# A state-space scan: seven of sixteen states weighted in transposed form by ScalarE, VectorE's own states written over their decays

## What is computed

```python
dt = softplus(dt_low @ W_dt + b_dt)
A = -exp(A_log)                                  # (512, 16)
def step(h, inputs):                             # h: (4, 512, 16)
    dt_t, x_t, B_t, C_t = inputs
    h = exp(dt_t[..., None] * A) * h + (dt_t * x_t)[..., None] * B_t[:, None, :]
    y = einsum('bds,bs->bd', h, C_t)
    return (h, y)
y = (scan of step over 1024 tokens) + x * D
y = y * silu(z)
```

## Time and profile before

| | us |
|---|---|
| median of three runs | 4037.8 |
| lowest and highest run | 4034.0 and 4038.71 |
| the profiled execution | 4035.95 |
| its span, from the first to the last instruction | 4034.2 |

### The profile page before, as it was taken

One profiled execution on the slowest core, in us unless ns is written; L12 is line 12 of the kernel. 1 busy time (PEld: TensorE's weight loads), 2 busy tenths in 40 slices (PEclk: granted clock), 3 DMA queues, 4 the chain that ended last, 5 costly groups with the idle time before them and its releaser, 6 DMA issues. The chain is left out here.

```text
span 4034.2 us, 46003 instructions
## 1 busy us (share of the span) xinstructions
PE 3270.3 (81%) x16080; PEld 1802.9 (45%) x16080; DVE 2552.3 (63%) x3494; ACT 1604.3 (40%) x2988; POOL 1605.5 (40%) x1002
## 2 busy tenths in 40 slices
PE   8599997588888799789888798895466777667894
PEld 5244442355555455455555455332122222224773
DVE  8588884465665422365665322487799999997633
ACT  2277776155555311255555211355233333332100
POOL 4100000333333211233333211255799999995503
PEclk9799999699999899899999899998788888888897
DMA  5955550600000311100000321243615151512574
GB/s 161 138 68 68 68 68 28 200 17 21 17 21 21 105 54 47 55 17 21 19 19 17 87 63 61 89 143 127 252 46 214 52 219 45 216 52 97 188 217 122
DMA packets 286671, 356.64 MB, mean 88 GB/s; under 512 B 71940, under 2 KB 218220, under 8 KB 285804
## 3 DMA queue, kind: packets, MB, share of 16 engines
q1 hardware_dynamic: 272636, 329.96, 29.2%
q10 hardware_dynamic: 10736, 15.38, 1.1%
q0 software_dynamic: 3072, 8.39, 0.7%
HBM read 245.63 MB, written 107.48 MB: 88 GB/s over the span
## 5 line engine op out<-in xcount | busy, mean ns | idle before, releaser
L2265 POOL TENSOR_TENSOR H_feed<-H_ndu,H_bs 128x1024 f32<-128x1024 f32 x256 | 593.8, 2349 | 8.4 <-DMA H_cs<-between_bc 8.3
L2247 ACT ACTIVATE H_decay<-H_ndt,H_rate 128x1024 f32<-128x1024 f32 x256 | 286.2, 1118 | 548.8 <-DVE H_state L2319 460.0
L2348 PE MATMUL H_p_y<-H_part,H_minus 128*128 128x512 f32 x704 | 380.6, 672 | 133.1 <-DVE H_part L2296 133.0
L2319 DVE TENSOR_TENSOR_SCAN H_state<-H_decay,H_feed 128x1024 f32<-128x1024 f32 x176 | 404.5, 2298 | 49.7 <-POOL H_feed L2265 25.6
L709 ACT ACTIVATE B_probs<-B_p_exp,B_key_bias 128x512 f32<-128x512 f32 (+3 forms) x768 | 392.6, 582 | 107.6 <-PE B_p_exp L753 77.4
L643 DVE TENSOR_REDUCE B_part_max<-B_p_max 128x1 f32<-128x512 f32 (+3 forms) x768 | 375.3, 546 | 90.3 <-PE B_p_max L730 87.7
L1230 ACT ACTIVATE D_probs<-D_scores,D_neg,D_rq 128x256 f32<-128x256 f32 x512 | 281.6, 564 | 237.5 <-DVE D_neg L1148 237.5
L1089 POOL TENSOR_TENSOR D_rnorm<-D_norm,D_power 128x8 f32<-128x8 f32 x64 | 106.1, 1658 | 633.7 <-DVE D_norm L1107 633.7
L2348 PEld LDWEIGHTS H_p_y<-H_part,H_minus 128*128 128x128 f32 x704 | 140.5, 209 | 352.9 <-DVE H_part L2296 201.8
L727 PE MATMUL B_p_max<-B_k,B_q 100*128 100x512 bf16 (+3 forms) x768 | 255.1, 338 | 39.1 <-DMA B_key_bias<-in_key_bias 32.8
L1644 PE MATMUL E_p_ag<-E_hT,E_w 128*128 128x512 f32 x640 | 283.6, 603 | 2.0 <-ACT E_hT L1600 2.0
(11 more groups left out here) (256 smaller groups left out, 6702.4 us busy)
## 6 DMA issues: line engine op xcount, KB each, us to landing
H_bs<-between_bc SPq DMA_DIRECT2D x64, 512.0 KB, 9.6
H_cs<-between_bc SPq DMA_DIRECT2D x64, 512.0 KB, 11.1
B_q<-between_q_parts SPq DMA_DIRECT2D x96, 128.0 KB
B_k<-between_k_parts SPq DMA_DIRECT2D x96, 128.0 KB
D_base<-between_z SPq DMA_DIRECT2D x64, 128.0 KB, 2.2
between_z<-D_z SPq DMA_DIRECT2D x64, 128.0 KB, 1.7
E_rest<-between_z SPq DMA_DIRECT2D x16, 512.0 KB, 5.2
between_sz<-F_sz SPq DMA_DIRECT2D x8, 1024.0 KB, 4.2
```

Of the source, the lines that this page charges most:

```text
L2247: nc.scalar.activation(decay[:, n % 2, :], ndt[:, g % 2, :], ACT.Exp, scale=rate[:, m, s:s + 1]).then_inc(decayed, 1)
L2265: nc.gpsimd.tensor_tensor(feed[:, n % AHEAD, :], ndu[:, g % 2, :], bs[:, s, :], ALU.mult).then_inc(fed, 1)
L2319: nc.vector.tensor_tensor_scan(out, decay[:, n % 2, :], feed[:, n % AHEAD, :], 0.0, ALU.mult, ALU.add).then_inc(scanned, 1)
L2348: last = nc.tensor.matmul(p_y[:, c, :], minus[:, :], src[:, c * CHUNK:(c + 1) * CHUNK], start=False, stop=s == NS - 1)
```

## The change

The sixteen states of a tile now fall into three classes, by the string `CLASS = "TTDPTDTDPTDTPDTD"`: six D, three P, seven T.

- P (3, 8, 12) is what was called shared: scan to `handed`, product by GpSimd.
- D (2, 5, 7, 10, 13, 15) is VectorE's own. Its scan writes over the decay that it reads, `decay[:, n % 2, :]` in PSUM, and its product comes at once behind it. The tile `state` is gone. Decay n therefore waits for the product of n-2, where n-2 is a D.
- T (0, 1, 4, 6, 9, 11, 14): the scan goes to `turning` in SBUF, in three buffers. TensorE turns its eight 128x128 blocks into `p_T`, two banks of PSUM (`turn`). ScalarE copies them to `sT` with a scale per partition, which is now time, taken from C turned (`weigh`, eight ACTIVATEs of 128x128). TensorE multiplies each with `minus` as the moving operand, which turns it back, and adds it to `p_y` (`bring`, eight matmuls of 128 columns).

C for that is loaded once for each sequence as 16 rows of 1024 (`load_c`, 64 KB), turned by TensorE (`turn_c`, eight small transposes) and copied by ScalarE (`put_c`) in the last tile of the sequence before. Only the nine rows of C that are not T's are still spread to 128 partitions. The one semaphore `summed` becomes three, one for each class. TensorE's queue gets a new order: at step n the sum of P n-4, `bring` of T n-2, the sum of D n-1, `turn` of T n; the skip term comes with the first sum of its tile. On ScalarE the weighing of n-2 stands behind decay n. The tail now stands behind the scan of state 1.

```diff
+        CLASS = "TTDPTDTDPTDTPDTD"
-        cs = a.sb("cs", [P, NS, SEQ])
+        cs = a.sb("cs", [P, len(weighted), SEQ])
+        c_rows = a.sb("c_rows", [NS, SEQ])
+        cT = a.sb("cT", [P, 2, NB, NS])
+        turning = a.sb("turning", [P, 3, SEQ])
+        sT = a.sb("sT", [P, 2, NB, P])
-        state = a.ps("state", [P, SEQ])
+        p_T = a.ps("p_T", [P, 2, HB, P])
...
+            def weigh(n):
+                g, s = units[n]
+                i, k = g // XT, before["T"][n]
+                act.wait_ge(copied, 2 * use_of_c(i) + 2)
+                if k >= 2:
+                    act.wait_ge(t_summed, k - 1)
+                for h in range(2):
+                    act.wait_ge(turned, 2 * use_of(n) + h + 1)
+                    for b in range(HB):
+                        last = nc.scalar.activation(sT[:, k % 2, h * HB + b, :], p_T[:, h, b, :], ACT.Copy,
+                                                    scale=cT[:, i % 2, h * HB + b, s:s + 1])
+                    last.then_inc(copied, 1)
...
-                reached(act, scanned, n - 1)
+                if n >= 2 and kind[n - 2] == "D":
+                    act.wait_ge(parted, before["D"][n - 1])
+                else:
+                    reached(act, scanned, n - 1)
                 nc.scalar.activation(decay[:, n % 2, :], ndt[:, g % 2, :], ACT.Exp, scale=rate[:, m, s:s + 1]
                                      ).then_inc(decayed, 1)
+                if n == 1:
+                    put_c(0)
+                if n >= 2:
...
+                    if kind[n - 2] == "T":
+                        weigh(n - 2)
...
-                nc.vector.tensor_tensor(part[:, k % 3, :], state[:, :], cs[:, s, :], ALU.mult).then_inc(parted, 1)
+                nc.vector.tensor_tensor(part[:, k % 3, :], decay[:, n % 2, :], cs[:, weighted.index(s), :], ALU.mult
+                                        ).then_inc(parted, 1)
...
+                elif kind[n] == "T":
+                    if k >= 3:
+                        dve.wait_ge(turned, 2 * use_of([j for j in range(n) if kind[j] == "T"][k - 3]) + 2)
+                    out = turning[:, k % 3, :]
                 else:
+                    out = decay[:, n % 2, :]
                 nc.vector.tensor_tensor_scan(out, decay[:, n % 2, :], feed[:, n % AHEAD, :], 0.0,
                                              ALU.mult, ALU.add).then_inc(scanned, 1)
+                if kind[n] == "D":
+                    times_c(n)
-                if g and s == 2:
+                if g and s == 1:
                     tail(g - 1)
...
+            def turn(n):
+                u, k = use_of(n), before["T"][n]
+                pe.wait_ge(scanned, n + 1)
+                for h in range(2):
+                    pe.wait_ge(copied, 2 * u + h - 1)
+                    for b in range(HB):
+                        at = (h * HB + b) * P
+                        last = nc.tensor.transpose(p_T[:, h, b, :], turning[:, k % 3, at:at + P], ident[:, :])
+                    last.then_inc(turned, 1)
+
+            def bring(n):
+                g, s = units[n]
+                skip_term(g)
+                k = before["T"][n]
+                for h in range(2):
+                    pe.wait_ge(copied, 2 * use_of(n) + h + 1)
+                    for b in range(HB):
+                        last = nc.tensor.matmul(p_y[:, h, b * P:(b + 1) * P], sT[:, k % 2, h * HB + b, :], minus[:, :],
+                                                start=False, stop=False)
+                last.then_inc(t_summed, 1)
...
+            for n in range(NU + 5):
+                if 0 <= n - 4 < NU and kind[n - 4] == "P":
+                    k = before["P"][n - 4]
+                    pe.wait_ge(pool_parted, k + 1)
+                    add(n - 4, pool_part[:, k % 2, :], p_summed)
+                if 0 <= n - 2 < NU and kind[n - 2] == "T":
+                    bring(n - 2)
+                if 0 <= n - 1 < NU and kind[n - 1] == "D":
+                    k = before["D"][n - 1]
+                    pe.wait_ge(parted, k + 1)
+                    add(n - 1, part[:, k % 3, :], d_summed)
+                if n < NU:
+                    i = units[n][0] // XT + 1
+                    if units[n] == (XT * i - 1, NEXT_C) and i < SEQS:
+                        turn_c(i)
+                    if kind[n] == "T":
+                        turn(n)
```

More of the change, by code:

```diff
@@ L2140, in phase_scan @@
         NU = len(units)
-        shared = [s % 3 == 1 for g, s in units]
-        shared_before = list(accumulate(shared, initial=0))
-        own_before = [n - k for n, k in enumerate(shared_before)]
+        CLASS = "TTDPTDTDPTDTPDTD"
+        NB = SEQ // P
+        HB = NB // 2
+        NEXT_C = CLASS.index("P", NS // 2)
+        kind = [CLASS[s] for g, s in units]
+        before = {c: list(accumulate((k == c for k in kind), initial=0)) for c in "TDP"}
+        per = {c: CLASS.count(c) for c in "TDP"}
+        weighted = [s for s in range(NS) if CLASS[s] != "T"]
+        row_bytes = [16 if CLASS[s] == "T" else 32 for s in range(NS)]
         AHEAD = 4
@@ L2180, in reached, with use_of, use_of_c @@
                 eng.wait_ge(sem, value)
+        def use_of(n):
+            i = units[n][0] // XT
+            return before["T"][n] + 1 + i + (n % (XT * NS) > (XT - 1) * NS + NEXT_C and i + 1 < SEQS)
+        def use_of_c(i):
+            return before["T"][(XT * i - 1) * NS + NEXT_C] + i if i else 0
         @block.sync
@@ L2229, in _ @@
                     load_tail(g + 1)
+                if m == 0 and i + 1 < SEQS:
+                    load_c(i + 1)
                 if m == XT - 1 and i + 1 < SEQS:
@@ L2281, in _ @@
                     feeds(n)
-                if n >= 2 and shared[n - 2]:
+                if n >= 2 and kind[n - 2] == "P":
                     shared_product(n - 2)
@@ L2291, in times_c @@
                     dve.wait_ge(row_loaded[s], 32 * (i + 1))
-                k = own_before[n]
+                k = before["D"][n]
+                reached(dve, d_summed, k - 2)
                 dve.wait_ge(scanned, n + 1)
-                if k >= 3:
-                    dve.wait_ge(summed, [j for j in range(n) if not shared[j]][k - 3] + 1)
-                nc.vector.tensor_tensor(part[:, k % 3, :], state[:, :], cs[:, s, :], ALU.mult).then_inc(parted, 1)
+                nc.vector.tensor_tensor(part[:, k % 3, :], decay[:, n % 2, :], cs[:, weighted.index(s), :], ALU.mult
+                                        ).then_inc(parted, 1)
@@ L2331, in _ @@
         def _(pe):
[L2332 to L2346 removed]
+            started = set()
@@ new lines, in skip_term, with turn_c @@
+            def skip_term(g):
+                if g in started:
+                    return
+                started.add(g)
+                reached(pe, yg_ready, g)
+                pe.wait_ge(tail_loaded[g % 2], 32 * (g // 2 + 1))
+                for c in range(2):
+                    nc.tensor.matmul(p_y[:, c, :], skip_diag[:, tiles[g][1], :],
+                                     xs[:, g % 2, c * CHUNK:(c + 1) * CHUNK], start=True, stop=False)
+            def turn_c(i):
+                u = use_of_c(i)
+                pe.wait_ge(c_loaded, 16 * (i + 1))
+                for h in range(2):
+                    if u:
+                        pe.wait_ge(copied, 2 * u + h - 1)
+                    for b in range(HB):
+                        at = (h * HB + b) * P
+                        last = nc.tensor.transpose(p_T[:, h, b, 0:NS], c_rows[:, at:at + P], ident[0:NS, 0:NS])
+                    last.then_inc(turned, 1)
@@ L2347, in _, with add @@
+            def add(n, src, done):
+                g, s = units[n]
+                skip_term(g)
                 for c in range(2):
@@ L2349, in _ @@
                                             start=False, stop=s == NS - 1)
-                last.then_inc(summed, 1)
+                last.then_inc(done, 1)
+            pe.wait_ge(fixed, 48)
+            pe.wait_ge(diag_ready, 1)
+            turn_c(0)
+            for n in range(NU + 5):
[13 more added lines that the diff above has]
+                        turn_c(i)
+                    if kind[n] == "T":
+                        turn(n)
 EXPERTS = 32
```

80 lines of the change are left out of this document (40 added, 40 removed).

## The result

| | before | after |
|---|---|---|
| median, us | 4035.90 (4 runs) | 3928.52 (4 runs) |
| lowest and highest run | 4028.51 and 4038.71 | 3916.73 and 3932.89 |
| the profiled execution | 4035.95 | 3929.91 |
| its span | 4034.2 | 3928.1 |
| mean granted clock of TensorE | 0.918 | 0.942 |

The ratio is 0.9732, 95% interval 0.9713 to 0.9751. Of the 106.0 us between the two profiled executions 105.1 lie in the scan: from the start of the first scan (2856.84) to the end of the last tail (3586.99) it is 730.2 us, where it was 835.3. The forecast had 98.8 there (3590.2 - 2853.7 = 736.5 us for the stage) and 1.8 more ahead of the first scan, 100.6 in all.

A forecast was written before the change was run, and what follows sets the result against it. VectorE's (DVE's) own queue bounds the scan stage. 2853.7 + 16 x 44.4 + 15 x 1.35 + 1.5 + 4.3 = 3590.2 instead of 3690.8; 4035.95 - 100.6 + 1.9 = 3937 us, range 3926 to 3972.

The forecast's parts named there:

- a product followed by a scan 1.34 to 1.36: VectorE's queue: start-to-start time in us, read from the earlier timeline, that a product holds the queue before a scan.
- like a product: VectorE's queue: the tail, standing between two scans, should hold the queue 1.35 us.
- Cost 0; its cover is gone to a tenth.: GpSimd: feed 15 ready at 42.0, when scan 15 starts; 0.5 us per tile if an operation takes 0.04 more.
- The walk: GpSimd's queue followed through a tile: product 3 at 11.9, feed 15 thirteenth at 2.31 us each, ready at 42.0.
- first rival: GpSimd becomes the bound: 1 to 2 us per tile, 3953 to 3969 us; chance 0.17.
- The second rival: ScalarE holds decays back: 3.5 us weighings give 3951, table loads at each change 4015; chance 0.08.
- at 2.9 per weighing it is 11.7: ScalarE, states 0 and 1: with 2.9 us weighings decay 4 is done at 11.7, just when wanted; cost 0.
- The third rival: TensorE loses its clock at the tile's border: 4091 us, half about 4010; chance 0.06 whole, 0.05 part.
- The fourth rival: Transposes don't hold TensorE's clock; work after gaps before `bring` 4 and 9 starts low: 3959 us; chance 0.07.
- The fifth: D scan in place in PSUM pays the high end, 7.3 us per tile: 4054 us; chance 0.03.
- The wait at the third feed: Stage start: third feed at 2857.2 us leaves VectorE 1.5 us of the 2.8 it waited there.
- the longer end: Stage end: last product to last tail 4.3 us instead of 3.4, with `bring` 14 and the last sum in line.

The follow-up runs named there:

- late product: GpSimd's product of a P state placed one feed later in its queue (behind feed n+3 instead of n+2), against the changed kernel: 3908.14 us, ratio 0.9688.
- longer weighing: Twelve ACTIVATEs instead of eight per weighing, the extra four into an unread tile, against the kernel with the late product: 3997.58 us, ratio 0.9895.
- the run with the turnings moved: Kernel with the longer weighing, each turning from state 2 on put ahead of `bring` n-2 and the D sum in TensorE's queue: 3997.85 us, ratio 0.9908.
- all turnings moved: Nine-T kernel (two P, five D, late product), turnings from state 2 on put ahead of `bring` n-2 and the D sum: 4021.24 us, ratio 0.9965.

## Why the prediction was right

Forecast 3937, measured 3928.5; the range 3926 to 3972 holds it. The step from the engines' shares to DVE's queue as the price of the tile was right, and so was what leaves that queue. Two terms were off, in opposite directions, and that the time lies in the range is in part luck: with DVE's queue as it was measured and no wait for POOL it is 3908 (the run with the late product), below 3926.

**DVE's queue.** Forecast 45.75 us per tile, measured 44.27 where nothing else binds (the late product). The term that was mis-sized is "a product followed by a scan 1.34 to 1.36": the number was read rightly in the earlier trace rows, but there each own scan had to wait for the product that read `state`. The change takes this wait away, since a scan now writes elsewhere, and a product or a tail holds the queue 1.14 and 1.12 us. Seven times 0.21 is 1.5 us per tile. The list of waits before hardly named it, 0.5 us in the whole stage, its gaps being too short; the run with the wait put back showed what it costs there, 0.28 us each time. The trace before had both numbers side by side, right behind the tail of the earlier trace rows at 3021.40:

```profile
3022.52 1.21 DVE L2296 TENSOR_TENSOR H_part<-H_state,H_cs 128x1024 f32<-128x1024 f32 x1
3023.87 2.30 DVE L2319 TENSOR_TENSOR_SCAN H_state<-H_decay,H_feed 128x1024 f32<-128x1024 f32 x1
```

The product of state 2 does not wait for the tail and starts 1.12 us behind it; the scan waits for the product and starts 1.35 us behind it. The prediction gave the tail 1.35, "like a product". The prediction counted what the change removes in instructions, and missed what it removes in waits between two instructions of one engine.

**POOL.** "Cost 0; its cover is gone to a tenth." The walk named the place, the scan of state 15, and the chain, the product of state 3 and twelve operations behind it, rightly. With a slower DVE it even holds: with the wait put back, at 46.3 us per tile, POOL's wait is gone. With DVE faster it binds, 0.87 us per tile. This is the first rival's mechanism, smaller than its low end of 1 us, and a consequence of the first error: 44.26 + 0.87, and two waits of 1.4 for a decay in fourteen tiles, is 45.3, the measured tile. The forecast was too high by 0.49 us per tile, 7 us in fourteen. A walk with a margin of a tenth should have been given a chance nearer to a half than to 0.17.

**ACT and table loads.** 387 ns an ACTIVATE against 366, 2.15 us a weighing against 2.3, one table load in the stage: the mechanism held and the terms balance. The second rival fell. The runs with more T's and with a longer weighing show that the walk's verdict on its margins was too kind: "at 2.9 per weighing it is 11.7" allowed 0.6 us more for nothing, and 1.0 us more costs 5.3 us per tile. That this comes by way of PE's queue is how the waits read; the run with the turnings moved did not bear it out, so the cause is open.

**PE.** 86% busy in the stretch and 0.98 of the clock: upper level, as taken. The third rival fell for this kernel; waits that pull the clock down do show in the runs with the longer weighing and with all turnings moved. `bring` takes 1.95 us instead of 1.8, and the skip term's records are 605 ns on average instead of 1082 before. The fourth rival's mechanism is there, at one place and with nothing behind it that DVE needs. The fifth fell, 2280 ns.

**Start and end.** In this execution the phase began 3.8 us later, and the first scan came 1.3 later, so 2.5 sooner by the phase (forecast 1.8). The wait at the third feed is 2.41 us (forecast 1.5), and with it and POOL's waits within the first tile the first tail stands 52.2 us behind the first scan (50.3). From the fifteenth tail to the end it is 44.2 us (45.7). Of this, from the start of the last product to the end of the last tail it is 4.6, where the sum had 1.35 + 4.3 = 5.65: the tail waits 2.13 us for PE, as it did before (2.15), so the longer end that the forecast added for `bring` 14 and the last sum did not come. Together with the tiles, -6.9 + 2.0 - 1.4 = -6.3, which is what the stage is shorter than forecast. With the first scan 3.1 us later than forecast and 2.2 us less behind the stage the profiled execution is 5.4 under its forecast of 3935.4; that it lies 1.4 above its median, and the 1.9 added for the median before, make up the rest of the 8.5.

## What to carry to other kernels

Before you take a start-to-start time from a trace, ask which wait is inside it and whether the change keeps that wait; here a scan that had to wait for the product before it cost 0.2 to 0.3 us each time, and the list of waits before hardly showed it. Where a walk of a second engine has no margin, move its optional work back in the queue before measuring (here one line, 0.5%). In an in-order queue look at what is ready behind a wait: the turning, moved ahead at one state where its scan was done, brought 20 us, and moved ahead at nearly all of them, where it waited with ready work behind it, cost 90.

## What the runs showed of the hardware that I had not expected

- A VectorE product of 128x1024 with both operands in SBUF, beside a busy GpSimd, takes 2447 ns on average (mostly 1.34 to 3.24 us) instead of 1225 with one operand in PSUM, and GpSimd's feeds, which also read two tiles of SBUF, go from 2364 to 2662 ns. With GpSimd idle the same product takes 1.22 us.
- A scan that writes over its own input in PSUM costs no more than one into SBUF, 2280 and 2274 ns.
- A product that the next scan need not wait for holds VectorE's queue 1.14 us of its 1.23; with a wait for its end it is 1.42.
- In the run with the longer weighing no engine is busy over 90% of the stretch (79 to 89%), and each waits for another, with PE's granted clock at 0.95; moving the turnings ahead changed none of the time.
